# Cross-attention with group norm on one core: one statistics product per batch, its arithmetic on GpSimd, small matrices in two slots, rounding one step ahead

## The reference

```python
q = (Wq @ ctx + bq).reshape(8 heads, 16, 1024)      # k likewise with Wk, bk
v = (Wv @ x + bv).reshape(8, 16, 1024)
scores = einsum('hdl,hel->hde', q, k) / sqrt(128)
out = einsum('hde,hel->hdl', softmax(scores), v).reshape(128, 1024)
o = Wo @ out + bo[:, None] + x
o_hat = (o - mean(o)) * rsqrt(var(o) + 1e-5)        # mean and variance over all 128 x 1024
return o_hat * gn_w[:, None] + gn_b[:, None]
```

## Time and profile before

| | before |
|---|---|
| median of 3 runs | 174.3 us (174.11 to 174.43) |
| the profiled execution, whole | 174.09 us |
| its span, first to last instruction | 172.3 us |
| mean granted TensorE clock | 0.982 |
| busy share PE, DVE, ACT, POOL | 94%, 88%, 79%, 65% |
| transfers | 50.83 MB, mean 295 GB/s |

### The profile page before, as it was taken

One profiled execution on the slowest core, in us unless ns is written; L12 is line 12 of the kernel. 1 busy time (PEld: TensorE's weight loads), 2 busy tenths in 40 slices (PEclk: granted clock), 3 DMA queues, 4 the chain that ended last, 5 costly groups with the idle time before them and its releaser, 6 DMA issues. The chain is left out here.

```text
span 172.3 us, 3697 instructions
## 1 busy us (share of the span) xinstructions
PE 161.3 (94%) x997; PEld 128.1 (74%) x997; DVE 150.8 (88%) x555; ACT 136.7 (79%) x356; POOL 112.5 (65%) x166
## 2 busy tenths in 40 slices
PE   7989999999999999999999999999999999999720
PEld 7777888777777788887777777888877777776410
DVE  1796999999999999999999999999999999977541
ACT  3656588988888888889888888888899888776342
POOL 3287677778777777777787777777777787731010
PEclk9999999999999999999999999999999999999975
DMA  5999778899989999999989999899999865633233
GB/s 198 416 402 372 261 226 305 331 339 327 334 331 345 364 318 332 310 338 335 331 312 338 343 352 359 307 327 337 327 336 332 297 234 230 246 123 124 122 122 122
DMA packets 14276, 50.83 MB, mean 295 GB/s; under 512 B 1712, under 2 KB 1712, under 8 KB 14256
## 3 DMA queue, kind: packets, MB, share of 16 engines
q1 hardware_dynamic: 13968, 50.34, 80.4%
q10 hardware_dynamic: 288, 0.27, 0.5%
HBM read 33.82 MB, written 16.78 MB: 294 GB/s over the span
## 5 line engine op out<-in xcount | busy, mean ns | idle before, releaser
L509 PE MATMUL o_ps<-x_sb,m_sb 128*128 128x512 f32 x128 | 63.0, 614 | 0.0
L426 DVE TENSOR_TENSOR hl_sb<-y_sb,hl_sb 128x512 fp32r<-128x512 f32 x64 | 47.1, 737 | 0.8 <-ACT hl_sb L321 0.8
L266 POOL TENSOR_TENSOR rstd<-veps,nhalf 128x1 f32<-128x1 f32 x32 | 28.3, 885 | 23.2 <-DVE veps L431 23.2
L321 ACT CAST hl_sb<-y_sb 128x512 fp32r<-128x512 f32 x64 | 39.6, 622 | 1.9 <-DMA y_sb<-in_ctx_dram 1.9
L509 PE MATMUL g_ps<-hl_sb 128*128 128x258 f32 x256 | 38.6, 293 | 0.0
L361 ACT ACTIVATE out_sb<-o_ps,shift,gain 128x1024 f32<-128x1024 f32 (+1 forms) x32 | 38.3, 1198 | 0.1
L295 POOL TENSOR_TENSOR lsuma<-hl_sb 128x256 f32<-128x256 f32 x31 | 23.2, 749 | 22.8 <-DVE hl_sb L426 22.8
L509 PEld LDWEIGHTS o_ps<-x_sb,m_sb 128*128 128x128 f32 x128 | 21.8, 191 | 14.8 <-issue 14.8
L509 PEld LDWEIGHTS g_ps<-hl_sb 128*128 128x128 f32 x256 | 32.8, 190 | 0.0
L457 DVE BATCH_NORM_STATS2 bn<-o_ps 128x6 f32<-128x512 f32 x32 | 22.4, 699 | 4.1 <-PE o_ps L509 0.5
L316 ACT ACTIVATE a_sb<-sc_sb,smin 128x128 f32<-128x128 f32 x32 | 12.9, 403 | 16.0 <-DVE smin L417 15.9
(11 more groups left out here) (64 smaller groups left out, 297.8 us busy)
## 6 DMA issues: line engine op xcount, KB each, us to landing
y_sb<-in_ctx_dram SPq DMA_DIRECT2D x32, 512.0 KB, 5.0
x_sb<-in_x_dram SPq DMA_DIRECT2D x32, 512.0 KB, 5.4
out_dram<-out_sb SPq DMA_DIRECT2D x31, 512.0 KB, 4.8
out_dram<-out_sb SPq DMA_DIRECT2D x2, 256.0 KB, 2.2
w_in<-in_weights_dram ACTq DMA_DIRECT2D x1, 256.0 KB, 5.7
cols<-in_columns_dram ACTq DMA_DIRECT2D x1, 3.0 KB, 3.4
```

Source lines behind the costliest of these rows:

```text
L266: nc.gpsimd.tensor_tensor(rstd[:, h1:h1 + 1], veps[:, h1:h1 + 1], nhalf[:, :], ALU.pow).then_inc(rstd_ready, 1)
L321: nc.scalar.copy(hl_sb[:, k, chunks, 0:C], y_sb[:, k, chunks, :]).then_inc(h_ready, 1)
L426: nc.vector.tensor_tensor(hl_sb[:, ky, chunks, C:2 * C], y_sb[:, ky, chunks, :], hl_sb[:, ky, chunks, 0:C].bitcast(F32), ALU.subtract).the ...
L509: return nc.tensor.matmul(dst, lhsT, rhs, start=start, stop=stop, **more)
```

## The change

Per batch there is now one statistics product of three columns, `statistics`, in place of the mean and the variance product. It sums the deviations and their squares about a pivot, and the pivot of the next batch, which is made beforehand from the first column of x (`pivot_column`). VectorE copies the product's result to SBUF (`copy_statistics`), and GpSimd works out the variance, the shift and the inverse deviation from the copy. On VectorE `fold_matrix` takes the place of L410 and also sums the rows of M. Small matrices have two slots each. ScalarE works one step further on in its list: its step t+1 goes with step t of the others, and it rounds half 0 of batch t at the end of its step t. The order of all lists is new. The low sums of the first two batches are made by TensorE, those of the first one before. The last batch has its own PSUM room and its own arithmetic on VectorE, and its two half stores are issued by two engines.

The core of the diff (new orders and new functions; removed lines stand in the kernel above):

```diff
-EARLY = 1
+EARLY = 2
-FILL = 2
+FILL = 1
+        @block.sync:    load_y(b) x4; for t: load_y(t + 3); load_x(t); store(t - 5)
...
+        # gpsimd
+            def negative_variance(b):
+                pool.wait_ge(stc_ready, b + 2)
+                nc.gpsimd.tensor_tensor(msq[:, h:h + 1], stc[:, h, 0:1], stc[:, h, 0:1], ALU.mult).then_inc(msq_ready, 1)
+                pool.wait_ge(msq_ready, b + 1)
+                nc.gpsimd.tensor_tensor(nvar[:, h:h + 1], msq[:, h:h + 1], stc[:, h, 1:2], ALU.add).then_inc(nvar_ready, 1)
+            def variance(b):
+                pool.wait_ge(nvar_ready, b + 1)
+                nc.gpsimd.tensor_scalar(veps[:, h:h + 1], nvar[:, h:h + 1], -1.0, EPS, ALU.mult, ALU.add).then_inc(veps_ready, 1)
+            def shift_by_pivot(b):
+                pool.wait_ge(stc_ready, b + 1)
+                pool.wait_ge(m_copied, b + 1)
...
+                nc.gpsimd.tensor_tensor(cp[:, b % 2:b % 2 + 1], m_sb[:, b % 2, E:E + 1], stc[:, (b + 1) % 2, 2:3],
+                                        ALU.add).then_inc(cp_ready, 1)
+            def weighted_shift(b):
...
+                pool.wait_ge(cp_ready, b + 1)
+                nc.gpsimd.tensor_tensor(wshift[:, h:h + 1], stc[:, h, 0:1], cp[:, h:h + 1], ALU.add).then_inc(wshift_ready, 1)
+            for t in range(B + LAGS):
+                fold_first(t - 1)
+                fold_second(t - 1)
+                fold_sum(t - 1)
+                fold_last(t - 1)
+                negative_variance(t - 4)
+                variance(t - 4)
+                shift_by_pivot(t - 3)
+                weighted_shift(t - 4)
+                inverse_deviation(t - 4)
...
+        # scalar
+            for t in range(B + LAGS + 1):
+                exponential(t - 4)
+                scale_bk(t - 3)
+                normalise(t - 4)
+                scale(t - 6)
+                copy_r(t - 4)
+                offset(t - 6)
+                output(t - 6)
+                round_half(t - 1, 1)
+                if t == 1:
+                    bias_rows()
+                copy_cross(t - 2)
+                round_half(t, 0)
...
+        # vector
+            def fold_matrix(b):
+                dve.wait_ge(m_ready, b + 1)
+                nc.vector.tensor_tensor_reduce(out=m_sb[:, b % 2, 0:E], in0=m_ps[:, 0:E], in1=ident[:, 0:P], scale=1.0,
+                                               scalar=0.0, op0=ALU.add, op1=ALU.add, accum_out=colsum[:, b % 2:b % 2 + 1])
+                nc.vector.tensor_tensor(m_sb[:, b % 2, E:E + 1], m_ps[:, E:E + 1], bo, ALU.add).then_inc(m_copied, 1)
+            def pivot_column(b):
...
+                nc.vector.scalar_tensor_tensor(out=st_in[:, (b + 1) % 2, 2:3], in0=colsum[:, b % 2:b % 2 + 1],
+                                               scalar=x_sb[:, b % SLOTS, 0:1], in1=m_sb[:, b % 2, E:E + 1],
+                                               op0=ALU.mult, op1=ALU.add).then_inc(pivot_ready, 1)
+            def copy_statistics(b):
+                dve.wait_ge(st_ready, b + 2)
...
+                nc.vector.tensor_copy(stc[:, b % 2, part], st_ps[:, part]).then_inc(stc_ready, 1)
+            for t in range(B + LAGS):
+                invert_sum(t - 3)
+                rest_half(t - 1, 1)
...
+                add_gram(t - 2)
+                statistics_of(t - 4, 0)
+                statistics_of(t - 4, 1)
+                aggregate(t - 4)
...
+                add_query_bias(t - 2)
+                deviation(t - 4)
+                fold_matrix(t - 3)
+                square(t - 4)
+                pivot_column(t - 3)
+                minimum(t - 2)
+                copy_statistics(t - 4)
+                rest_half(t, 0)
+                copy_sum(t - 1)
+            last_output()
...
+        # tensor
+            def statistics(b):
...
+                    pe.wait_ge(q_ready, b + 1)
...
+                    pe.wait_ge(pivot_ready, b + 2)
...
+                    product(st_ps[:, part], onesn[:, :], st_in[:, b % 2, part]).then_inc(st_ready, 1)
+            for t in range(B + LAGS):
+                input_product(t - 4, 0)
+                input_product(t - 4, 1)
+                softmax_product(t - 3)
+                query(t - 2)
+                gram(t - 1, 0)
+                value_product(t - 3)
+                gram(t - 1, 1)
+                scores(t - 2)
+                statistics(t - 4)
+                transpose_cross(t - 1)
```

More of the change, by code:

```diff
@@ L40, in xattn_groupnorm_kernel @@
     P = 128
-    assert E == P and C == P and L % (4 * P) == 0 and B % UNROLL == 0
+    assert E == P and C == P and L % (4 * P) == 0 and B % SLOTS == 0
     DH = E // HEADS
@@ L515, in keep_busy, with gram @@
                     product(o_ps[:, 1, 0:P], onesn[:, :], onesn[:, :])
+            def gram(b, half):
+                if not live(b):
+                    return
+                pe.wait_ge(l_ready, 2 * b + 1 + half)
+                if half == 0 and b >= 1:
+                    pe.wait_ge(g_copied, b)
+                    pe.wait_ge(s_copied, b)
+                for c in range(half * HCH, (half + 1) * HCH):
+                    mm = product(g_ps[:, 0:HL], hl_sb[:, b % SLOTS, c, 0:C], hl_sb[:, b % SLOTS, c, :],
+                                 start=(c == 0), stop=(c == CH - 1))
+                if half == 1:
+                    mm.then_inc(hl_ready, 1)
@@ new lines, in transpose_cross @@
+            def transpose_cross(b):
+                if not live(b):
+                    return
+                pe.wait_ge(b2_copied, b + 1)
+                transposed = product(g_ps[:, 0:C], b2_sb[:, b % 2, :], ident_r[:, :], start=False, skip_group_check=True)
+                if b < EARLY:
+                    for c in range(CH):
+                        low = product(early_ps[:, 2 * b:2 * b + 2], hl_sb[:, b, c, C:2 * C], ones_r[:, :],
+                                      start=(c == 0), stop=(c == CH - 1))
+                    low.then_inc(g_ready, 1)
+                else:
+                    pe.wait_ge(lsum_ready, b - EARLY + 1)
+                    product(g_ps[:, 2 * C:HL], lsum[:, b % 2, :], ones_r[:, :], start=False,
+                            skip_group_check=True).then_inc(g_ready, 1)
```

721 lines of the change are left out of this document (388 added, 333 removed).

## The result

The changed kernel takes 197.41 us, median of 4 runs (197.17 to 199.91), the kernel before beside it 174.21 us (174.05 to 174.43). The ratio is 1.136, with a 95% interval of 1.127 to 1.146. The profiled execution took 197.62 us with a span of 195.7. The forecast was 186.8 us, with a range up to 197: the direction was right, and the forecast growth of 12.7 us was little more than half of the 23.5 that came.

What follows compares the result with a forecast made beforehand. The prediction took TensorE to bound the kernel before at 4.74 us a step and GpSimd's list, 5.23, the changed one: 174.1 + 29 x (5.23 - 4.74) - 1.5 = 186.8 us, range 178 to 197 us.

Steps and rivals of the forecast that it cites:

- TensorE's part: TensorE's queue set the 4.74 us step; removing the variance product saves 0.25 us, leaving 4.49 us of its own work.
- ScalarE's ring: Loop of TensorE and ScalarE through softmax product, copy_r, output, rounding half and cross copy: no step under 4.99 us.
- GpSimd's list: GpSimd's adds, small operations and power, 4.39 us plus 0.84 of lock-outs: 5.23 us a step, the bound; chance 0.46.
- the lock-outs: VectorE's rest halves shut out GpSimd's small operations: 0.38 us lost on msq and 0.46 on nvar.
- Rival 2: Longer ring through GpSimd, ScalarE's scale waiting for the power ahead of copy_r: 5.5 to 5.6 us, 196.1 us; chance 0.13.
- The sign that I had named for it: In the trace, ScalarE waiting for GpSimd's power ahead of r_sb would show the longer ring through GpSimd.
- Rival 3: GpSimd and VectorE lock held for whole instructions, each lock-out 0.14 us longer: step 5.51, 194.9 us; chance 0.04.
- VectorE's part: VectorE's list: 4.67 us of work a step, 4.97 with the whole wait for the statistics product.
- Start and end: First output product some 0.5 us earlier, last batch saves the mean's round: together -1.5 us, between -3 and +1.
- the clock is no rival: TensorE's clock was said to stay at its upper level, 2.4 GHz, judged from 160 to 165 us.
- The sum: Whole time from the profiled execution, 29 steps and the ends: 174.1 + 29 x (5.23 - 4.74) - 1.5 = 186.8 us.
- The rule on the lock: Skill's rule that GpSimd and two-SBUF-input VectorE instructions exclude each other; trace agreed, but the second enters 0.14 us early.

Runs made afterwards that it cites:

- e4: Kernel before, with ScalarE's shift moved behind the copy of r_sb and its second rounding half ahead of the cross copy; 193.25 us.
- e1: Changed kernel, with ScalarE copying r_sb before it scales the gain; 200.47 us.
- i3: h_old_scalar_order with VectorE's statistics arithmetic behind a rest half and the s_sb copy, and ScalarE's sbk_sb and r_sb ahead of gain; 183.06 us.
- e2: Changed kernel, with VectorE's deviation and pivot taking one tensor input and per-partition scalars instead of two tensor inputs; 194.70 us.
- h_old_scalar_order: Changed kernel with arithmetic on VectorE, one-tensor deviation and pivot, filling products at the start, and ScalarE's list in the kernel before's order; 185.96 us.
- f4: Changed kernel, with the statistics arithmetic done by VectorE from PSUM instead of by GpSimd; 189.14 us.
- f1: Changed kernel with r_sb copied before the gain, one-tensor deviation and pivot, and the second rounding half behind the cross copy; 203.61 us.
- f2: Changed kernel, with five filling products behind each of TensorE's steps 0, 1 and 2 instead of one behind steps 1 and 2; 195.38 us.

## Why the prediction was right and wrong

**TensorE's part.** TensorE was the bound before and is none after: it now waits in each step, and the product's 0.25 us went nowhere, since each of the other limits is longer than the old step.

**ScalarE's ring, 4.99 us.** Right as a lower bound for the changed kernel's order. e4 shows it alone (5.43 against a price of 5.46), e1 and i3 show it with `gain` in it. It was never the longest in the changed kernel.

**GpSimd's list.** The small operation was priced at 0.21 us and takes 0.19. The list was priced at 5.23 and measured 5.40 when it was the bound (e2). The term that was too small is the lock-outs: I had 0.38 on `msq` and 0.46 on `nvar`, together 0.84; they fell on `msq` (0.68 to its successor against 0.29, so 0.39) and on `veps` (0.82 against 0.16, so 0.66), 1.05 in all. The second rest half starts 0.95 us after the copy in after (96.39 to 97.34), not 0.82 as I had it, and so in the steady step catches the third operation in place of the second.

**The step that failed** is the choice of the bound. Rival 2, a longer ring through GpSimd, was described with its members and priced at 5.5 to 5.6 us and 196.1 in all, and it is what happened (5.40 steady, 5.49 in the mean, 197.4). I gave it 0.13 and the list 0.46. I had its sum on paper, even if added up too high: its terms, 4.16 and lock-outs of 0.38, 0.46 and 0.45, make 5.45 and not 5.5 to 5.6, which would have been 193.2 us. Either is more than 5.23, and of two limits the longer one rules whatever one thinks of the other. The sign that I had named for it, ScalarE waiting for the power ahead of `r_sb`, is the longest wait of after. I had discounted the ring for containing three uncertain lock-outs, yet two of the three stood in the forecast too; the third, on the pivot (0.47 against 0.22 undisturbed), was there, and a fourth that I didn't have, on the deviation (0.56 against 0.15), held up `fold_matrix`, since these follow each other on VectorE. The list's 5.40 in e2 is another limit of the same size: it has other members, and in after GpSimd waits 0.26 us ahead of `msq`.

**Rival 3**, the lock held for whole instructions, was priced near the measured mean (5.51), but is not what happened: in after `msq` ends at 97.20 us, 0.06 behind the rest half (97.14), where it takes 0.19 by itself, so it got in some 0.13 us before the rest half ended; and e2's list is 5.40, not 5.51, with both lock-outs in it.

**VectorE's part.** 4.67 of work and a wait of 0.3, 4.97 in all, stands against 4.80 of work and a step of 5.08 in h_old_scalar_order, with the arithmetic on VectorE. In the changed kernel it was hidden, as forecast.

**Start and end.** The end came as priced: 1.1 us less against 0.9, since one hand-over to TensorE and back is gone: from the last `bn_aggr` to the output 2.78 us pass (188.84 to 191.62) where before had 3.50 (164.81 to 168.31). Timeline of after:

```profile
189.08 0.16 DVE L583 TENSOR_TENSOR st_in<-mv,cp 128x1 f32<-128x1 f32 x1
...
191.62 0.81 DVE L617 TENSOR_SCALAR out_sb<-ps_ps,gain,shift 128x512 f32<-128x512 f32 x1
```

Here the deviation takes 0.16 us, as `dev` did, since GpSimd does nothing beside it: the 0.56 of the steady state is lock-out. The start had the wrong sign: +2.7 against -0.5. Two things failed: "the clock is no rival" rested on a window of the end, where TensorE had been busy for 150 us, and said nothing of the start; and the query product, which I had as removed from the path, came onto it.

**The sum again with what was measured:** 174.1 + 29 x (5.49 - 4.74) + 2.7 - 1.1 = 197.5 us, against 197.6. The forecast's shortfall of 10.8 is 29 x 0.26 = 7.5 of step and 3.1 of start and end, and rounding. Either miss alone would have left the time inside the range: 194.4 us with the measured steps and the forecast's -1.5, 189.9 with its steps and the measured start and end.

**The rule on the lock.** The Trainium skill, SBUF — State Buffer, section "SBUF: two separate sides", has GpSimd and a VectorE instruction with two SBUF inputs exclude each other. The traces of after and e2 agree: 0.56 and 0.47 against 0.15 and 0.22 undisturbed in the same form, and 0.21 and 0.27 in the middle of an add in the form with one SBUF tensor. The warning of Perfetto Trace Analysis, section "Optimizing Scalar/DVE Operations", that moving work between the two might not help, came true with 8.3 us for the arithmetic (f4 against after). The shared port, which the page gives as the reason, is only part of it here: of the 2.04 us from the copy to the power's start the two lock-outs are 0.70 (0.57 and 0.51 against 0.19 each).

## What to carry to other kernels

In an ordered software pipeline, list every closed loop through the queues, price each, and forecast the longest, not the best understood one; a loop with uncertain terms is not shorter for that. An instruction of little weight (a 128x1 gain, a shift) can set the step when it waits for a far engine and something of the next batch stands behind it: the same arithmetic cost 5.40 or 6.13 us a step by where two small operations stood. When a change opens one limit and nothing moves, look for the next of equal length before calling the theory false: four lay between 4.9 and 5.4 us here.

## What the runs showed of the hardware

A small VectorE operation on [128 x 1] that reads two SBUF tensors is shut out by a GpSimd add as a large one is: 0.56 us in place of 0.15, and 0.47 in place of 0.22 (after); in the form with per-partition scalars it takes 0.21 and 0.27 in the middle of an add (e2). The same lock-out costs a GpSimd add of 128x128 0.54 us when a rest half starts with it (0.99 in place of 0.45, f1). A GpSimd operation of 128x1 takes 0.19 us, 0.14 to 0.15 from start to start, and 0.5 to 0.75 when a rest half goes beside it. TensorE's clock was at half (0.50, 1.2 GHz) in one stretch of the start with TensorE busy all of it (2.00 of 2 us from 16 to 18 us in after), and at full (1.00) in the same stretch of f2, where TensorE had been busy 4.64 of 5 us between 5 and 10 us in place of 3.58.
